# Two-layer attention and feed-forward network on one core: attention and the last ternary layer joined into one stage

## The reference

```python
x = x + L1_xattn(LN(x), ctx_2048, ...)       # 16 heads of 128; its last step: out @ o_w + o_b
# _L1_ffn_ref(LN(x), weight, bias):
scale = jnp.mean(jnp.abs(weight))
w_t = jnp.clip(jnp.round(weight / (scale + EPS)), -1.0, 1.0)
x = x + jnp.einsum('bsi,oi->bso', LN(x), w_t * scale) + bias
```

## Time and profile before

| | |
|---|---|
| Median of 3 runs | 1530.53 us (1530.34 to 1531.22) |
| The profiled execution's own time | 1529.64 us |
| Its span | 1527.9 us |
| TensorE busy | 1375.9 us, 90% of the span |
| VectorE, ScalarE, POOL busy | 831.7, 762.5, 426.1 us |
| Mean granted TensorE clock | 0.941 of full speed |

### The profile page before, as it was taken

How to read it: one execution, slowest core, us unless ns; L and a number is a source line. 1 busy time by engine, 2 the same in 40 slices (tenths; PEclk the granted TensorE clock), 3 DMA queues, 4 the chain that set the end, 5 groups by cost and what they waited for, 6 DMA issues and landing times. The chain is left out here.

```text
span 1527.9 us, 25936 instructions
## 1 busy us (share of the span) xinstructions
PE 1375.9 (90%) x7406; PEld 1142.0 (75%) x7407; DVE 831.7 (54%) x1534; ACT 762.5 (50%) x1858; POOL 426.1 (28%) x379
## 2 busy tenths in 40 slices
PE   6899998999898969979998938999958899999979
PEld 5786676888777759867876627878857788888867
DVE  2432332467666775434444237824258877777845
ACT  4222223588678736125555544545436466566541
POOL 0110102236363900438923033120059200000031
PEclk9999998799999977989999978999969999999989
DMA  6998245888787710247554775563436455555402
GB/s 237 353 353 316 110 139 175 290 280 256 232 259 238 249 63 28 110 161 224 181 164 142 237 241 159 172 229 131 159 115 182 116 160 165 155 166 158 112 35 110
DMA packets 172052, 281.17 MB, mean 184 GB/s; under 512 B 29824, under 2 KB 64384, under 8 KB 171712
## 3 DMA queue, kind: packets, MB, share of 16 engines
q1 hardware_dynamic: 147120, 227.85, 46.8%
q0 software_dynamic: 7712, 26.22, 5.2%
q10 hardware_dynamic: 17136, 26.09, 4.6%
HBM read 173.40 MB, written 106.70 MB: 183 GB/s over the span
## 5 line engine op out<-in xcount | busy, mean ns | idle before, releaser
L2530 ACT ACTIVATE attend_prob<-banks,attend_row,rq 128x128 f32<-128x128 f32 x256 | 113.7, 454 | 69.9 <-DVE attend_row L2589 69.9
L100 PE MATMUL banks<-of_shared_split,heads_wl 128*128 (+1 forms) x256 | 109.5, 428 | 19.6 <-ACT heads_ksq L944 14.5
L100 PE MATMUL banks<-of_shared_split,of_ctx_lead 128*128 128x512 f32 x256 | 106.4, 416 | 9.3 <-DVE of_ctx_trail L419 5.5
L100 PE MATMUL banks<-attend_wol,attend_ol 128*128 (+1 forms) x256 | 106.4, 416 | 0.0
L100 PE MATMUL banks<-of_x_lead,queries_wl 128*128 128x512 f32 x256 | 101.3, 396 | 4.1 <-ACT queries_sq L2183 2.6
L102 PE MATMUL banks<-of_shared_split,heads_wt 128*128 (+1 forms) x256 | 103.6, 405 | 0.0
L101 PE MATMUL banks<-of_shared_split,heads_wl 128*128 (+1 forms) x256 | 103.3, 404 | 0.0
L102 PE MATMUL banks<-of_shared_split,of_ctx_trail 128*128 128x512 f32 x256 | 103.0, 402 | 0.0
L101 PE MATMUL banks<-of_shared_split,of_ctx_lead 128*128 128x512 f32 x256 | 102.9, 402 | 0.0
L102 PE MATMUL banks<-attend_wol,attend_ot 128*128 (+1 forms) x256 | 101.0, 394 | 0.0
L102 PE MATMUL banks<-of_x_lead,queries_wt 128*128 128x512 f32 x256 | 100.5, 392 | 0.0
(11 more groups left out here) (339 smaller groups left out, 3645.2 us busy)
## 6 DMA issues: line engine op xcount, KB each, us to landing
mlstm_gmax<-running_max SPq DMA_DIRECT2D x36, 512.0 KB, 6.0
heads_raw<-in_L_xattn_ki_w SPq DMA_DIRECT2D x32, 512.0 KB, 6.1
k_heads<-heads_key ACTq DMA_DIRECT2D x64, 256.0 KB, 4.6
q_heads<-queries_head SPq DMA_DIRECT2D x64, 256.0 KB, 2.4
attend_q<-q_heads SPq DMA_DIRECT2D x64, 256.0 KB, 4.2
of_attend_k<-k_heads SPq DMA_DIRECT2D x60, 256.0 KB, 4.1
of_attend_v<-v_heads SPq DMA_DIRECT2D x60, 256.0 KB, 3.3
sorted_rows<-values_zeros SPq DMA_DIRECT2D x2, 5120.0 KB, 18.2
```

The costliest lines, as they stand in the source:

```text
L100: nc.tensor.matmul(out, lead_l, lead_r, start=first, stop=False)
L2530: ins = nc.scalar.activation(prob[:, j % 2, b, :], ps[:, j % 2, b * S:(b + 1) * S], ACT.Exp, bias=row[:, j % 2, 1, b:b + 1], scale=rq[:, b ...
```

## The change

Both stages become one phase, `attend_and_last`, with one exit. Leads and trails go into the memory of the split output weights (group g's onto heads 4g to 4g + 3), the ternary weights into that of q. The first set of transposes stands between output products 2 and 3 of the last iteration, the second behind output product 3. On VectorE the trails of set 0 stand behind the statistics of the third late batch (b == 2), and the normalisation of the late batches behind the reciprocal, ahead of the trails of set 1. On ScalarE the leads of set 0 stand ahead of the late square root. The weights are loaded once all scores are made; the bias only once. POOL adds the bias batch by batch and waits for its own last add before each. Products 2 and 3 of group 0 wait for the adds of output products 2 and 3, whose banks they take. The diff, cut:

```diff
-def attend(nc, K, A, L, q_dram, k_dram, v_dram, rq, rk_dram):
+def attend_and_last(nc, K, A, L, q_dram, k_dram, v_dram, rq, rk_dram, tern_dram, out):
+        lead, trail = (w[:].rearrange("p (g c) n -> p g c n", g=G) for w in (wol, wot))
+        ternT = q[:].bitcast(F32R)
...
             sp.dma_start(tern_bias[:], L.bias_dram.partition_broadcast(P)).then_inc(tern_bias_loaded, 16)
+            sp.wait_ge(scores, IT * 4)
+            sp.dma_start(ternT.rearrange("p c d -> p (c d)").bitcast(F32), tern_dram).then_inc(tern_loaded, 16)
+            for b in range(B):
+                sp.wait_ge(y_done, b + 1)
+                sp.dma_start(out[b], K.x[:, b, :]).then_inc(stored, 16)
+            sp.wait_ge(stored, 16 * B)
...
             for g in range(G - 1):
-                pool.wait_ge(normal_done, (g + 1) * GB)
                 for b in range(g * GB, (g + 1) * GB):
-                    ins = nc.gpsimd.tensor_tensor(K.x[:, b, :], K.x[:, b, :], tern_bias[:], ALU.add)
-                ins.then_inc(tern_bias_done, 1)
-            pool.wait_ge(tern_bias_done, G - 1)
+                    pool.wait_ge(normal_done, b + 1)
+                    if b:
+                        pool.wait_ge(tern_bias_done, b)
+                    nc.gpsimd.tensor_tensor(K.x[:, b, :], K.x[:, b, :], tern_bias[:], ALU.add).then_inc(tern_bias_done, 1)
+            pool.wait_ge(staged, 1)
+            for b in range(EARLY, B):
+                pool.wait_ge(tern_bias_done, b)
+                nc.gpsimd.tensor_tensor(K.x[:, b, :], K.x[:, b, :], tern_bias[:], ALU.add).then_inc(tern_bias_done, 1)
...
+            def leads(g):
+                for c in range(C):
+                    act.wait_ge(rows_turned, g * C + c + 1)
+                    nc.scalar.activation(lead[:, g, c, :], ps[:, c, :], ACT.Copy).then_inc(lead_done, 1)
+
+            leads(0)
             act.wait_ge(late_agg, 1)
             nc.scalar.activation(K.rstd[:, late], K.mv[:, late, 1], ACT.Sqrt, bias=K.eps5[:, 0:1]).then_inc(late_root, 1)
-            act.wait_ge(normal_done, EARLY)
+            for g in range(1, G):
+                leads(g)
...
+            def finish(g):
+                for b in range(g * GB, (g + 1) * GB):
+                    dve.wait_ge(product, b + 1)
+                    dve.wait_ge(tern_bias_done, b + 1)
+                    nc.vector.scalar_tensor_tensor(K.x[:, b, :], ps[:, 4 + b % GB, :], L.scale[:, 0:1], K.x[:, b, :],
+                                                   ALU.mult, ALU.add).then_inc(y_done, 1)
+
             for b in range(GB):
                 add(IT - 1, b)
                 dve.wait_ge(acc_done, FIRST + (IT - 1) * GB + b + 1)
                 row_stats.batch(EARLY + b)
+                if b == 2:
+                    trails(0)
...
             dve.wait_ge(late_inverted, 1)
+            for b in range(EARLY, B):
+                ins = nc.vector.tensor_scalar(L.normal[:, b, :], K.x[:, b, :], K.mv[:, b, 0:1], K.rstd[:, b:b + 1],
+                                              ALU.subtract, ALU.mult)
+            ins.then_inc(staged, 1)
+            trails(1)
+            for g in range(G):
+                finish(g)
+                if g + 2 < G:
+                    trails(g + 2)
...
             def turn_rows(g):
                 if g == G - 1:
                     pe.wait_ge(staged, 1)
+                else:
+                    pe.wait_ge(normal_done, (g + 1) * GB)
...
             def products(g):
                 pe.wait_ge(trail_done, (g + 1) * C)
                 for b in range(g * GB, (g + 1) * GB):
                     if g:
                         pe.wait_ge(y_done, b - GB + 1)
+                    elif b >= 2:
+                        pe.wait_ge(acc_done, FIRST + (IT - 1) * GB + b + 1)
...
-            turn_rows(0)
+            for b in range(GB):
+                output(IT - 1, 1, b)
+                if b == 2:
+                    turn_rows(0)
+            turn_rows(1)
             pe.wait_ge(tern_loaded, 16)
-            turn_rows(1)
             for g in range(G):
                 products(g)
                 if g + 2 < G:
                     turn_rows(g + 2)
```

More of the change, by code:

```diff
@@ L2425, in attend @@
         normal_done, tern_bias_loaded, tern_bias_done = sem("normal_done"), sem("tern_bias_loaded"), sem("tern_bias_done")
+        tern_loaded, staged, rows_turned, lead_done, trail_done, product, y_done, stored = (
+            sem("tern_loaded"), sem("staged"), sem("rows_turned"), sem("lead_done"), sem("trail_done"),
+            sem("product"), sem("y_done"), sem("stored"))
         early, late = slice(0, EARLY), slice(EARLY, B)
@@ L2646, in _, with trails @@
             add(IT - 2, 3)
+            def trails(g):
+                for c in range(C):
+                    dve.wait_ge(lead_done, g * C + c + 1)
+                    nc.vector.tensor_tensor(trail[:, g, c, :], ps[:, c, :], lead[:, g, c, :].bitcast(F32), ALU.subtract
+                                            ).then_inc(trail_done, 1)
+            def finish(g):
[4 more added lines that the diff above has]
+                                                   ALU.mult, ALU.add).then_inc(y_done, 1)
             for b in range(GB):
@@ L2723, in _ @@
             output(IT - 2, 0, 3)
[L2724 to L2800, removed]
@@ L2816, in products @@
                         pe.wait_ge(y_done, b - GB + 1)
-                    r = slice(b * S, (b + 1) * S)
+                    elif b >= 2:
+                        pe.wait_ge(acc_done, FIRST + (IT - 1) * GB + b + 1)
+                    r = slice(b % GB * S, (b % GB + 1) * S)
                     for c in range(C):
-                        nc.tensor.matmul(ps[:, GB + b % GB, :], lead[:, c, r], ternT[:, c, :], start=(c == 0), stop=False)
-                        ins = nc.tensor.matmul(ps[:, GB + b % GB, :], trail[:, c, r], ternT[:, c, :], start=False,
+                        nc.tensor.matmul(ps[:, 4 + b % GB, :], lead[:, g, c, r], ternT[:, c, :], start=(c == 0), stop=False)
+                        ins = nc.tensor.matmul(ps[:, 4 + b % GB, :], trail[:, g, c, r], ternT[:, c, :], start=False,
                                                stop=(c == C - 1))
                     ins.then_inc(product, 1)
-            turn_rows(0)
+            for b in range(GB):
[3 more added lines that the diff above has]
+            turn_rows(1)
             pe.wait_ge(tern_loaded, 16)
-            turn_rows(1)
             for g in range(G):
@@ L2830, in _ @@
                     turn_rows(g + 2)
+class LastWeights:
+    pass
 class Routing:
@@ L2890, in two_layers @@
             L.normal = A.raw
-            attend(nc, K, A, L, q_dram, k_dram, v_dram, rq, rk_dram)
-            ternary(nc, K, L, tern_dram, out)
+            attend_and_last(nc, K, A, L, q_dram, k_dram, v_dram, rq, rk_dram, tern_dram, out)
 _INS = ['x', 'ctx_2048', 'L0_xattn_Wi', 'L0_xattn_bi', 'L0_xattn_Wf', 'L0_xattn_bf', 'L0_xattn_ln_scale',
```

4 lines of the change are left out of this document (2 added, 2 removed).

## The result

| | kernel before | changed kernel |
|---|---|---|
| Median | 1532.95 us (1530.34 to 1538.81, 6 runs) | 1521.42 us (1518.61 to 1524.92, 6 runs) |
| The profiled execution's own time, its span | 1529.64, 1527.9 us | 1524.92, 1523.1 us |
| Mean granted TensorE clock | 0.941 | 0.938 |

The ratio is 0.9931, 95% interval 0.9908 to 0.9954: 7 to 14 us faster. The forecast, 1518.1 against 1530.53, is a ratio of 0.9919 and lies inside that interval; but the measured time, 1521.42 us, lies 0.2 us above the range given (1515.8 to 1521.2). Direction and mechanism came out, the range did not.

What follows compares the result with a forecast made beforehand. TensorE sets the end, but POOL's bias additions hold the stage boundary. TensorE's path shortens 18.84 to 6.43 us, nothing else late: 1529.64 - 12.4 = 1517.2, plus 0.9 from profile to median, 1518.1 us; range 1515.8 to 1521.2.

Steps and rivals of the forecast that it cites:

- The sum on TensorE's path: From output product 2's end to the first ternary product's second matmul: 18.84 us becomes 6.43, 12.41 less.
- The exit: One exit with eight more semaphores at the kernel's end: no change, bounds -0.3 and +0.5 us.
- Trails of set 0: VectorE writes them by 1477.0, before transpose set 1 starts at 1477.36: slack 0.4 us for its first bank.
- the add of output product 3: On VectorE, moves from 1475.82 to 1477.56; trails queued ahead end at 1477.0 and cost it nothing.
- the two added waits: Ternary products 2 and 3 wait for adds met by 1473.8 and 1478.3, asked after 1482.6: no cost.
- the writes beside the reads of the output weights: Leads and trails of set 0 written while output product 3 reads other heads: nothing, bounds nothing to 2.7 us.
- POOL's waits: Waiting for its own last add costs POOL at most 0.08 us each; 12 adds end at 1481.2.
- Rival A: POOL holds VectorE's four late normalisations, 5.1 us in all; fifth product 2.3 us late, 1520.4 us; chance 0.05.
- The slack of 2.8 us: Batch 0's y is done at 1485.2; the fifth ternary product, taking its bank, wants it at 1488.0.
- Rival B: Clock falls at set 1: briefly, about 2 us, 1520; for all 128 products, 31 us, 1549; chance 0.02 each.
- Rivals C and D: C: ternary products still wait for staged, 1521.3 us, chance 0.03. D: stages stay apart, 1528 us, chance 0.01.
- D's price: At the stage boundary, cutting only the bias chain gains about 2.5 us, giving 1528 us; chance 0.01.

Runs made afterwards that it cites:

- before_no_bias: Kernel before without POOL's bias additions to the 12 early batches; from first TensorE start behind output product 2 to the end 49.46 us, against mean 54.9.
- bias_gate: Changed kernel, TensorE waiting ahead of set 1 for POOL's 12 early bias additions; from behind output product 2 to the end 49.89 us, +6.9.
- tern_late: Changed kernel with the ternary weights' load issued only after all output products; from behind output product 2 to the end 48.04 us, +5.0.
- normals_x3: Changed kernel with eight spare normalised batches written by VectorE ahead of the four needed; from behind output product 2 to the end 45.39 us, against 43.0.
- before_copy: Kernel before, run again unedited; ratio 0.9981 (0.9965 to 0.9998) to the kernel before; profiled execution 1531.96 us.

## Why the prediction was right or wrong

- **What bounded the kernel** came out: POOL's additions held the boundary (before_no_bias took 3.7 us out of the gap). Put back one by one into the changed kernel, the wait for POOL cost 6.9 us with its half clock (bias_gate) and the late load 5.0 (tern_late).
- **The sum on TensorE's path** was 12.41 us; 12.34 to the last y. The exit had been taken at no change with bounds of -0.3 and +0.5 us: it is +0.33 (3.94 instead of 3.61 us behind the start of the last y), shown in the traces, not by a run that isolates it. With both, the tail is 12.0 us shorter.
- **Trails of set 0, the add of output product 3, the two added waits, the writes beside the reads of the output weights:** all at nothing, as said. TensorE runs output product 3 at the old spacing (2.84 us from its first start to set 1, 2.80 forecast) while leads and trails are written. The forecast's slack of 0.4 us for the first bank of set 1 was too small: that bank waits for the first trail alone, which ended 2.3 us ahead (1482.33 against 1484.61).
- **POOL's waits** were mis-sized: I took 0.08 us each as the upper end, but 12 early additions took 17.12 us, so (17.12 - 12 x 1.30) / 11 = 0.14 us from one to the next. The four late ones, which wait only for POOL's own last add, took 5.41, so (5.41 - 4 x 1.29) / 3 = 0.08, the price I had. What I put at nothing is the early ones' second wait, for a normalised batch that had long been there: about 0.06 us by this difference, which no run isolates. POOL thus ended later than forecast and met the first two normalisations; covered by slack.
- **Rival A** had its mechanism right and its chain too long: holds of 0.3 and 1.0 us on two normalisations, not one of a whole add on each of four. The slack of 2.8 us less that hold left 1.5 by the forecast; normals_x3 gives 1.7.
- **Rival B** fell: with two sets of transposes around one output product the clock stayed at 1.00 in every window from 1440 to 1520. The Trainium skill's rule that transposes don't count for the clock (TensorE: Matmul & The Clock Gate, Part 4: PE-mode transpose) doesn't hold for the float32 transposes here: in before_no_bias the clock rose from 0.50 to full within 1486 to 1487, when 16 transposes were all that TensorE had done since the gap, and in before_copy it rose at about 1493.6, within the second set, ahead of the first ternary matmul at 1493.69. Idle alone did not raise it: it stayed at 0.50 from 1478.5 to 1483 in the kernel before. The trace calls the transposes MATMUL and doesn't tell whether they use the mode that the page means.
- **Rivals C and D** fell: no product waited for staged, and the stages did merge. D's price was too low: it gave about 2.5 us for cutting the bias chain alone, and before_no_bias gained 5.5.
- **The step that failed** is the one from the sum to the range. It read: "The forecast's own width is the slack of run against profile (0.9), the exit bounds and part of the operand bound". Three runs within 0.9 us, with the 3 us put as what a measurement can tell, were taken for the scatter of this program. That these three lay so close was luck: the next three of the same kernel were 1534.69 to 1538.81, and later sessions went from 1521 to 1537. The kernel before had a median of 1532.95 in the comparison; less the tail's 12.0 this is 1520.9, 0.5 us from the 1521.42 measured. Of the 3.3 us between 1518.1 and 1521.42, 2.4 are this move of the kernel before, 0.4 the difference of 12.4 and 12.0, and 0.5 is left. The change itself thus explains 0.4 us of the miss. The three medians of the changed kernel are 1521.42, 1515.29 and 1517.07 us, one above the range, one below it and one inside: where it came to lie was chance. A range of 1518.1 within 5 us would have held all three. The chances are hardly touched by it: against a scatter of some 8 us to either side of a single run, the interval of the ratio still lies below 1 in each of three comparisons.

What stays open is the cause of the scatter. It grows over the first 1200 us and not in one stage: in the thirteen traces, with the same instructions ahead, the first activation of L892 starts between 256.4 and 263.0 us, L1270 between 598.8 and 610.5 and the tail between 1467.2 and 1480.1. It goes with the granted clock: of the 60 runs of the kernel before in the three later sessions, the 21 with a mean clock of 0.936 or less average 1532.2 us and the 15 with 0.942 or more 1524.9. Whether the clock or the arrival of data is first wasn't tried.

## What to carry to other kernels

A boundary between stages costs more than its barrier: the slowest engine's leftover work, the loads that can only be issued behind it, and the half clock behind the gap; here 7.5 us of gap (3.7 of it POOL's work), 1.2 us for the load and 3.8 us at half clock, less 0.1 for the first matmul behind the set put in between. Before merging, list for every engine what it still has to do at the old boundary and when the next stage wants it, and put the first rows of the next stage into the last products of this one only as far as their evacuation needs cover (0.8 us here). Take the scatter of a program from many runs, and compare an unchanged stretch of two traces before reading a difference of two whole times.

## What the runs showed of the hardware

- TensorE's clock rose from half to full with float32 transposes as its only work since the gap (before_no_bias, before_copy). In before_no_bias 16 were enough; in the kernel before 16, a wait of 1.15 us and 16 more ran at half clock, and it rose at about 1491.6, 0.3 us behind them. The gap ahead was 7.4 us there and 3.7 in before_no_bias; no run isolates what sets the instant.
- A gap of 1.0 us left the clock at 1.00 (normals_x3); gaps of 3.2 us (tern_late), 3.7 (before_no_bias) and 4.4 (bias_gate) were each followed by a stretch at 0.50, which began between 2.2 and 4.0 us behind TensorE's last work, in tern_late and before_no_bias only after it had started again.
- A VectorE normalisation with all tensor data in on-chip memory waits for a POOL addition under way (four took 3.18 against 1.92 us; the held ones ended 0.28 to 0.29 us behind the addition), while additions that read a bank beside POOL kept 0.69 us.
